# Depooled rows gathered by indirect transfers that add into the token tile

## The reference

```
x = x + xattn(layernorm(x), ctx, patch_lens, ...)
x = x + moe(layernorm(x), gate_w, w1, w3, w2)

def xattn(embeds, patch_embeds, patch_lens, W_in, b_in, g_res, g_init):
    h = rmsnorm(embeds, g_res)
    h = einsum('bld,ed->ble', h, W_in) + b_in
    h_patch = rmsnorm(patch_embeds, g_init)[..., :256]
    s = scan over the patches: s[t] = a * s[t-1] + c * h_patch[t]
    plug[t] = which patch token t belongs to (from the patch lengths)
    return s[plug] + h
```

## Time and profile before

| What | Value |
|---|---|
| Time, median of 3 runs | 485.46 us (485.13 to 485.64) |
| Time of the profiled execution | 485.91 us |
| Its span | 484.2 us |
| TensorE matmul busy | 422.1 us (87%) |
| VectorE busy | 259.7 us (54%), 750 instructions |
| ScalarE busy | 192.6 us (40%) |
| GpSimd busy | 155.0 us (32%), 130 instructions |
| DMA | 33077 packets, 50.92 MB, mean 105 GB/s |
| GpSimd's own DMA queue (q0) | 8080 packets, 12.33 MB |
| GpSimd's gathers, line 443 | 16, 15.5 us in total |
| GpSimd's scatters that add, line 482 | 37, 78.3 us in total |
| GpSimd's gathers of the second part, line 474 | 40, 40.7 us in total |
| VectorE's additions, line 814 | 4, 1.22 us each |

### The profile page before, as it was taken

The page is one execution under the profiler, slowest core; times in us unless marked ns, Lnnn a source line. Parts: engine busy times, 40 slices in busy tenths (PEclk is TensorE's granted clock), DMA queues, the critical chain, the costliest instruction groups (busy, mean ns, idle before and its releaser), DMA issues.

```text
span 484.2 us, 10484 instructions
## 1 busy us (share of the span) xinstructions
PE 422.1 (87%) x2557; PEld 366.8 (76%) x2558; DVE 259.7 (54%) x750; ACT 192.6 (40%) x334; POOL 155.0 (32%) x130
## 2 busy tenths in 40 slices
PE   0768984329899999999999999999999999999980
PEld 0557864327688988888888888888988888888870
DVE  7977857988753355334553553365355334552230
ACT  3446444203442445324544443454445324542220
POOL 5354440022042234223432432253234223432321
PEclk9979886558999999999999999999999999999996
DMA  6856787400719112811136128112711211211121
GB/s 194 308 175 218 261 265 220 167 24 22 271 26 292 32 22 27 287 32 22 25 102 220 22 42 283 22 22 70 254 22 22 32 32 22 27 30 30 22 32 11
DMA packets 33077, 50.92 MB, mean 105 GB/s; under 512 B 3335, under 2 KB 25095, under 8 KB 33063
## 3 DMA queue, kind: packets, MB, share of 16 engines
q1 hardware_dynamic: 24983, 38.44, 23.6%
q0 software_dynamic: 8080, 12.33, 13.1%
HBM read 39.36 MB, written 11.40 MB: 105 GB/s over the span
## 4 chain that ended last, share of the span: by engine, by line
PE 73%; DVE 6%; issue 2%; DMA 2%; POOL 1%; DVEq 1%; ACT 0%; POOLq 0%; ACTq 0%
PE bank L1329 63%; PE bank L1352 6%; PE bank L1336 2%; DMA dg<-depool_rows,plugi 1%; DVE ctx_sb L904 1%; PE bank L1262 1%; DMA out<-yblk,itok 1%; PE bank L1283 1%; POOL dg L443 1%; DVE split L1124 0%; DVE split L323 0%; DVE batch L992 0%; PE bank L1208 0%; POOL out L482 0%; DVE onehot_lo L988 0%
## 5 line engine op out<-in xcount | busy, mean ns | idle before, releaser
L1329 PE MATMUL bank<-split,xT_hi 128*128 x592 | 166.8, 404 | 1.4 <-DVE xT_lo L1089 1.4
L1098 DVE TENSOR_TENSOR hmul<-gact,bank 128x512 f32<-128x512 f32 x74 | 50.9, 688 | 145.4 <-ACT gact L611 145.4
L482 POOL DMA_INDIRECT out<-yblk,itok x37 | 78.3, 2115 | 150.3 <-ACT yblk L618 138.3
L1329 PEld LDWEIGHTS bank<-split,xT_hi 128*128 128x128 f32 x592 | 106.9, 190 | 22.4 <-issue 2.2
L1329 PE MATMUL bank<-split,hT 128*128 (+1 forms) x888 | 115.7, 287 | 1.5 <-issue 0.8
L1329 PEld LDWEIGHTS bank<-split,hT 128*128 128x128 f32 x888 | 108.8, 192 | 2.1 <-issue 1.3
L611 ACT ACTIVATE gact<-bank 128x512 f32<-128x512 f32 x74 | 44.2, 597 | 158.1 <-PE bank L1329 158.1
L1329 PE MATMUL bank<-split,xT_lo 128*128 x296 | 93.2, 396 | 0.0
L474 POOL DMA_INDIRECT xblk<-z_rows,gidx x40 | 40.7, 1018 | 106.3 <-DVE gidx L1111 100.4
L323 DVE TENSOR_TENSOR split<-raw,split (+1 forms) x22 | 50.4, 2292 | 37.1 <-ACT split L317 35.9
L1329 PEld LDWEIGHTS bank<-split,xT_lo 128*128 128x128 f32 x296 | 56.0, 189 | 13.3
(11 more groups left out here) (184 smaller groups left out, 312.9 us busy)
## 6 DMA issues: line engine op xcount, KB each, us to landing
raw<-in_L_ffn_w SPq DMA_DIRECT2D x24, 1024.0 KB, 8.2
ctx_sb<-in_ctx SPq DMA_DIRECT2D x4, 1024.0 KB, 6.4
x_all<-in_x SPq DMA_DIRECT2D x4, 512.0 KB, 8.2
depool_rows<-gact SPq DMA_DIRECT2D x4, 512.0 KB, 3.0
out<-x_all SPq DMA_DIRECT2D x4, 512.0 KB, 4.6
z_rows<-z SPq DMA_DIRECT2D x4, 512.0 KB, 3.8
xblk<-z_rows,gidx POOLq DMA_INDIRECT x40, 2.8
out<-yblk,itok POOLq DMA_INDIRECT x37, 4.7
```

What stands on the lines that cost most here:

```text
L482: pool.indirect_dma_start(out[:, :], bass.IndirectOffsetOnAxis(ap=itok[:, q:q + 1], axis=0), yblk[:, q, :], None, compute_op=ALU.add).then ...
L1098: dve.tensor_tensor(hmul[:, cols], gact[:, cols], p_lin[part][:, :], ALU.mult)\
L1329: mm = pe.matmul(out_, xp, w_, start=start and n == 0, stop=stop and n == 2)
```

## The change

The tile `dg` is gone. The four transfers of `gather(b)` write to `x_all` itself and carry `compute_op=ALU.add`: each adds the 128 rows that it fetches to the token rows that lie there. VectorE's addition of line 814 is gone, and with it the semaphore `xd_ready`. VectorE still waits for the four transfers before line 820. GpSimd no longer waits for `xd_ready` ahead of the gathers of batches 2 and 3 (these kept a buffer of `dg` from being overwritten). It waits instead, in every batch, until the statistics (`mv1_ready`) and the normed tokens (`hn_ready`) of that batch have been made from `x_all`, since these must see the tokens before anything is added. Nine small tiles that shared their place with `dg` have places of their own. Lines behind the tiles move up by two, those in `second` by seven or more.

```diff
-        with ExitStack() as early:
-            ln_i = sb("ln_i", [P, B, CH], i32, early)
...
-        dg = sb("dg", [P, 2, TPB, D], f32)
+        ln_i = sb("ln_i", [P, B, CH], i32)
...
                 pool.wait_ge(s["plug_ready"], 1)
                 pool.wait_ge(dep_rows[b], 16)
-                if b >= 2:
-                    pool.wait_ge(s["xd_ready"], b - 1)
+                pool.wait_ge(s["mv1_ready"], TPB * (b + 1))
+                pool.wait_ge(s["hn_ready"], TPB * (b + 1))
                 for j in range(TPB):
                     n = b * TPB + j
-                    pool.indirect_dma_start(dg[:, b % 2, j, :], None, depool_dram[b][:, :],
-                                            bass.IndirectOffsetOnAxis(ap=plugi[:, n:n + 1], axis=0))\
-                        .then_inc(dg_in[b], 16)
+                    pool.indirect_dma_start(x_all[:, n, :], None, depool_dram[b][:, :],
+                                            bass.IndirectOffsetOnAxis(ap=plugi[:, n:n + 1], axis=0),
+                                            compute_op=ALU.add).then_inc(dg_in[b], 16)
...
                 dve.wait_ge(dg_in[b], 16 * TPB)
-                dve.wait_ge(s["hn_ready"], TPB * (b + 1))
-                flat = x_all[:, b * TPB:(b + 1) * TPB, :].rearrange("p j d -> p (j d)")
-                dve.tensor_tensor(flat, flat, dg[:, b % 2].rearrange("p j d -> p (j d)"), ALU.add)\
-                   .then_inc(s["xd_ready"], 1)
-                dve.wait_ge(s["xd_ready"], b + 1)
                 xb = x_all[:, b * TPB:(b + 1) * TPB, :]
```

More of the change, by code:

```diff
@@ L178, in build @@
         NBC = B * CH
-        with ExitStack() as early:
-            ln_i = sb("ln_i", [P, B, CH], i32, early)
[L181 to L188, removed]
-        dg = sb("dg", [P, 2, TPB, D], f32)
+        ln_i = sb("ln_i", [P, B, CH], i32)
+        ln_f = sb("ln_f", [P, 4, B, CH], f32)
+        keep = sb("keep", [P, 4 * NBC], f32)
+        ln_s = sb("ln_s", [P, 4, B, CH], f32)
+        ln_c = sb("ln_c", [P, 4, NBC], i32)
+        ln_t = sb("ln_t", [P, NBC], i32)
+        ln_b = sb("ln_b", [P, 4, NBC], i32)
+        ln_v = sb("ln_v", [P, 8, NBC], f32)
+        ln_p = sb("ln_p", [P, 3, NBC], i32)
         onehot_hi = sb("onehot_hi", [P, NBC, TPB], bf16)
@@ L240, in build @@
             ids_ready base_step affine_step sq_ready st1_ready mv1_ready vin_ready rs_ready nb1_ready
-            hn_ready tn_ready hnT_ready hp_ready depmm_ready dep_ready hmm_ready xd_ready x1_ready
+            hn_ready tn_ready hnT_ready hp_ready depmm_ready dep_ready hmm_ready x1_ready
             st2_ready mv2_ready vin2_ready rs2_ready nb2_ready z_ready tz_ready zT_ready logit_mm
```

## The result

The changed kernel takes 490.67 us (median of 6 runs, 489.12 to 491.61) against 485.50 us (485.13 to 485.83, 6 runs): the ratio is 1.0106, with a 95% interval of 1.0088 to 1.0124. It is slower by 5.2 us. Its times spread over 2.5 us, those of the kernel before over 0.7.

The account below looks back on a forecast made before the run. The chain is mostly TensorE's second part, untouched; the front part runs through a loop over batches holding GpSimd's gathers. 2.5 + 2.5 + 1.86 + 0.5 - 0.8 - 1.3 = +5.3 us gives 490.7 us, range 486.3 to 494.0 (8 in 10).

Parts of the forecast that it names:

- The loop over batches: Front part: gathers, power, `nb2`, `depooled`, store, next gathers form a loop; longer gathers of batches 1 and 2 cost +2.5 us each.
- 1.59 us per adding gather: GpSimd's issue, taken from the scatter of line 482, against 0.95 plain (1.01 for a batch's first): +2.5 us per batch.
- rival with no price on GpSimd: Adding costs GpSimd's gathers nothing: -0.7 us, 484.8; 11% together with the idle-GpSimd rival.
- rival that GpSimd's idle time absorbs it: GpSimd, busy 32%, absorbs the issue; only last landing and addition count, time 484.8; 11% together with the no-price rival.
- that of blocked gathers at 2.5 us each: Rival: four adding gathers in a row block GpSimd, about 2.5 us each: +19 us, about 504; 5%.
- many descriptors can be emitted before it shows: Skill's rule on GpSimd's DMA issue: descriptor generation is a small part, so GpSimd would pay next to nothing; the first rival.
- The gain: VectorE's four additions of line 814 go; only batch 3's is in the chain: -1.3 us.
- Batch 0 is hidden: Batch 0's +2.5 us on GpSimd, and VectorE's later second step, delay nothing: 0 us; 2.5 more if the cover were gone.
- 0.7 us to spare for the power of batch 2: GpSimd: batch 2's first-norm power ends at 38.7, before the gathers of batch 1 start at 39.48 on their table.
- The disturbance of +0.5: VectorE's `hp` of batch 2 overlaps batch 1's first gather by 1.05 us; half taken between bounds 0 and 1.05.
- The last landing: Batch 3's last gather lands in 4.7 us in place of 5.47: -0.8 us; bounds 3.7 and 6.7.
- the new waits cost nothing: GpSimd's waits before the gathers for statistics and normed tokens are met long before: 0 us.

Follow-up runs that it names:

- e6: Kernel before, with only the gathers of batches 1 and 2 adding and VectorE adding the others: 489.96 us, ratio 1.0102.
- e3: Kernel before, with GpSimd's power of the second norm between the second and third gather of batches 1 and 2: 483.47 us, ratio 0.9971.
- e1: Changed kernel without `compute_op`, so gathered rows overwrite the tokens: 480.74 us, with 36 blocks in place of 37, so only the front part can be read.
- e5: Kernel before, with only batch 0's gathers adding and its VectorE addition gone: 488.08 us, ratio 1.0066.
- e10: Kernel before, with only batch 0's gathers adding and the first 1 MB weight load issued with the second: 486.16 us, ratio 1.0025.
- e7: Kernel before, with only batch 3's gathers adding and VectorE adding the others: 484.98 us, ratio 0.9997.
- second profile: Profile of the changed kernel run once more, unaltered: 493.36 us in the one run.
- e9: Kernel before, with only the first 1 MB weight load moved, issued together with the second: 485.82 us, ratio 1.0018.
- e12: Kernel before, with VectorE adding the W_in product before the rows, and GpSimd's power between second and third gather of batches 1 and 2: 482.32 us, ratio 0.9945.
- e11: Kernel before, no adding transfer, with VectorE adding the W_in product first and the gathered rows after it: 483.70 us, ratio 0.9975.

## Why the prediction was right, and where it was not

The time (490.7 predicted, 490.67 measured) fits better than its working deserves. In the first profile, from the kernel before to the changed one, up to the start of line 820 of batch 3:

| Step | predicted | first profile |
|---|---|---|
| Start of the gathers of batch 1 | 0 | -0.64 |
| Gathers of batch 1 | +2.5 | +2.47 |
| Power of batch 0 to the gathers of batch 2 | 0 | +0.48 |
| Gathers of batch 2 | +2.5 | +2.37 |
| Power of batch 1 to the gathers of batch 3 | 0 | +0.03 |
| Gathers of batch 3, first to last | +1.86 | +1.80 |
| Disturbance by VectorE | +0.5 | 0 |
| Last landing | -0.8 | -1.64 |
| Addition of line 814 | -1.3 | -1.26 |
| Sum | +5.3 | +3.6 |

- *The loop over batches* held: e6 gave the +4.9 of its two turns, and e3, which only moves GpSimd's power of the second norm, brought the front part forward by 3.1 us.
- *1.59 us per adding gather* held at 1.57. e1 shows that the price is that of `compute_op`. The rival with no price on GpSimd would have been 484.8 us and is out, and with it the rival that GpSimd's idle time absorbs it; that of blocked gathers at 2.5 us each is out too, as none took over 1.73. So is the rule that the prediction took from the Trainium skill (DMA: Bandwidth & Descriptors, section Anatomy of one DMA — SWDGE (gpsimd) path), that many descriptors can be emitted before it shows: the issue grew by 0.6 us.
- *The gain* held at 1.26 us, and only batch 3's addition was in the chain.
- *Batch 0 is hidden* failed. The step that failed is "with 4.7 us they are there before VectorE is free for that batch": the last adding gather of batch 0 landed 7 to 9 us after its issue (VectorE gets it at 42.79 in the first profile, at 44.19 in the second), since it runs beside a weight load. Alone, batch 0 costs 3.1 us (e5); without the load beside it 0.3 (e10). In the changed kernel its cost largely overlaps with that of batch 1's gathers: in the first profile the variances of batch 0 are ready at 46.01, and GpSimd is free at the same time; in the second they hold the power until 47.49. The parts of e5, e6 and e7 add up to 8.0 us, and the whole costs 5.2.
- *0.7 us to spare for the power of batch 2* was used up in the first profile. The table of batch 1 was stored earlier (34.05 in place of 35.43 us), as TensorE was at its full clock sooner; the gathers could start only when the power had ended (38.66). GpSimd's wait there shrank from 3.28 to 0.19 us. In the second profile, with the table stored at 34.69, 1.20 us of it were left.
- *The disturbance of +0.5* was nothing: the gather at 38.84 runs beside line 795 (38.77 to 40.48) and takes 1.59 us.
- *The last landing* was 3.83 us in one profile and 5.41 in the other, -1.6 or -0.1 against 5.47, around the predicted -0.8.

The terms left out (+1.4 for batch 0 in the second profile) and those too high or too low (disturbance, clock, landing) cancel in the median. That part of the agreement is luck. The 0.48 us between the power of batch 0 and the gathers of batch 2 are not explained; the second profile has them too (store to gather 4.11 us in both), e6 with the same waits hasn't (3.78). They don't come from the adding, as e1 has them with plain gathers (4.21), nor from the store, which lands 3.0 us after its issue in the kernel before, in both profiles and in e6. The prediction's "the new waits cost nothing" is thus not shown to the last half microsecond.

## What to carry to other kernels

An adding transfer is cheap only if nothing waits behind its issue and its landing has slack: here the same four transfers cost 0 us in the last batch and 2.5 in a batch where a small operation stands behind them on GpSimd. Before moving work to an engine that looks idle, follow what is queued behind it, and look at what else the DMA engines carry when the transfer will land. And before one takes an addition off a chain by making a transfer do it, see whether another operation can be done during the wait: swapping two additions gave the same microsecond for nothing.

## What the runs showed of the hardware

- A gather of 128 rows of 1 KB that adds into SBUF takes 1.53 to 1.74 us of GpSimd, a plain one 0.94 to 1.09, where VectorE leaves them alone, and leaves 144 packets in place of 48.
- The last adding gather of batch 0 landed 7 to 9 us after its issue beside a 1 MB load (42.79 - 35.40, 43.33 - 35.41, 44.19 - 35.39). Without the load the four of e10 landed in 3.9 to 5.3 us, and the plain ones of e9 in 3.5 to 4.1, so without a load adding makes 0.3 to 1.2 us of it, 0.6 of that the longer issue. In the kernel before, the plain gathers of batch 0 (2.7 to 4.1 us) were issued before the load. The first plain gather of batch 1 there (39.48) met the load's last 2 us, as the load landed 5.8 us after its issue at 35.84, and landed in 3.4. No plain gather was issued right at the load's start, so how a plain one would fare there is not shown.
- An addition on VectorE with both operands in SBUF stretches a gather that GpSimd issues beside it. GpSimd of e12:

```profile
39.25 1.01 POOL L446 DMA_INDIRECT dg<-depool_rows,plugi  x1 [3.07 <-DMA depool_rows<-gact]
...
50.88 2.13 POOL L446 DMA_INDIRECT dg<-depool_rows,plugi  x1 [2.96 <-issue]
...
61.47 0.97 POOL L446 DMA_INDIRECT dg<-depool_rows,plugi  x1 [3.62 <-issue]
```

The gather at 50.88 starts with line 822 (50.83 to 52.11) and takes 2.13 us in place of 1.02. The adding gather at 38.69 of e6 above, beside the addition of batch 0 (37.93 to 39.15), takes 1.99. So do a plain gather of e9 (38.40, 1.60 us, beside an addition from 37.88 to 39.11) and one of e11 (52.31, 1.84 us). The operation of line 797 (795 after), with two operands in SBUF and a scalar, left the gather at 38.84 at 1.59 us in the changed kernel and the plain one at 38.84 at 1.04 in e10; in e5 the one at 39.72 beside it took 1.26 in place of 1.01. The Trainium skill (SBUF — State Buffer, section Who interferes with whom) lets a VectorE instruction with two SBUF inputs and a GpSimd instruction that reads SBUF exclude each other; the additions agree with it, line 797 for the most part doesn't.
- TensorE's clock came back at other times from run to run: the same logits in 2.70 us (granted clock 0.69) and 3.59 (0.50), the same 24 matmuls in 3.13 us and 4.63. A gain of 1 us ahead of such a place can vanish there (e7), or 1.0 us of one of 3.1 (e3, by its profile).
